# Loading the first feed-forward input tile ahead of the weight preparation instead of behind it

## The chip, the cores and the metric

One Trainium2 chip; the kernel runs on all 8 cores, each with 2 of the 16 sequences, and the cores don't talk to each other. The time is that of the slowest core, in microseconds (us) on the device. Each core has five engines: TensorE (PE, matmuls), VectorE (DVE), ScalarE (ACT), GpSimd (POOL) and SyncE (SP). In this kernel SyncE issues all loads and GpSimd all stores, each in the order of its program; an instruction that waits holds up all that follow it on its engine.

## The reference

The input X is (16, 2048, 1024) in float32. One attention layer is followed by a normalization, then by a three-block feed-forward part with 4-bit weights and LoRA, then by another normalization:

```python
x = _layernorm(x + attn(x, Wq, bq, Wk, bk, Wv, bv))     # causal, softmax over axis -2
# feed-forward: three blocks
w = q.astype(float32) / 7.5 - 1.0;  w = w * repeat(scale, 16, axis=1)      # dequantized weight
linear(x) = x @ w.T + bias + (x @ la.T) @ lb.T                             # LoRA of rank 32
h = x
for blk in range(3):
    y = gelu(layernorm(linear0(h)) * gamma + beta)
    h = linear1(y) + h
x = _layernorm(x + h)
```

## The kernel before, in words

One large buffer PL of 40,960 float32 columns per partition holds nearly everything; constants such as IBASE and O_WSTG are column offsets in it. Data is transposed: features on the partitions, tokens along the columns.

**Attention.** For each of the two sequences of a core: projections, scores, attention times values, residual sum. The stage ln1 then normalizes. Its result x1 (2048 tokens x 1024 features) lies in eight chunks of 128 x 2048 from offset 8192 on. VectorE normalizes chunks 0 to 4 (L624, L627) and GpSimd chunks 5 to 7 (L635, L638). After its own part GpSimd stores all eight chunks, 1 MB each, to the DRAM buffer x1s (L646). Where these stores stand is kept in sp_marks, one mark for each sequence.

**Weight preparation ("dequant").** dequant_w(w), for each of six weights: SyncE loads the LoRA factors (L666, L667), then for each of eight chunks c the quantized values (L693) and the scales (L696), 512 KB each. Three chunks are in flight: the loads of chunk c wait for VectorE's end of chunk c-3. ScalarE converts the integers (L713). TensorE makes the LoRA product of the chunk (L725, L727). VectorE multiplies by the scales (L739), adds the LoRA product (L743, L745), and GpSimd stores the finished bf16 chunk of 256 KB to the DRAM buffer weffs (L704). VectorE may write chunk c only when the store of chunk c-2 has landed, since the staging buffer has two places. The first loads of weight 0 wait for the last attention matmul, for the statistics of ln1 and for VectorE's count before it normalizes. They go to columns 24576 to 30720, which the x1 data (offsets 8192 to 24576) doesn't use.

**Feed-forward.** emit_group takes two tiles of 512 tokens each (t even and t odd). x1_load(t) loads a tile from x1s in eight DMAs of 256 KB (L801) into columns IBASE[t % 2] on. It waits for the last attention matmul or last use of the place, for sp_marks of both sequences, and for what it is given as extra. For tile 0 this is VectorE's end of the attention part, for tile 1 the end of dequant on all engines. w_load(j) loads prepared weight j, 2 MB in one DMA (L782). cast_in(t) makes the bf16 copy of the tile on VectorE (L815), which waits for the eight loads. y_mms makes the matmuls of a linear layer (L857) with statistics matmuls (L837, L839) between. It waits for the cast and the weight, and its bank guards make the third and fourth output block of the first tile wait for the end of dequant on VectorE.

Before the change the order on SyncE's queue around here is: all loads of dequant, x1_load(0), w_load(0), w_load(1), x1_load(1). VectorE's order is: normalization, dequant, cast of tile 0, cast of tile 1.

Of the kernel before, what the change touches and what calls it, by code (L numbers as in the profile page):

```python
# [72 lines left out]
def build_program():  # L73
# [23 lines left out]
    with ExitStack() as ctx:  # L97
# [42 lines left out]
        def inc(inst, name, n=1):  # L140
            cnt[name] += n
            inst.then_inc(sem[name], n)
            return cnt[name]

        def wt(e, name, v):
            e.wait_ge(sem[name], v)

        def chain(e, name):
            e.wait_ge(sem[name], cnt[name])
# [4 lines left out]
        def scope(name):  # L154
            sid, _ = nc.enter_named_scope(name, False)
            _scope_stack.append((name, sid))

        def escope():
            name, sid = _scope_stack.pop()
            nc.leave_named_scope(name, sid, False)  # L160
# [492 lines left out]
        attn_end = dict(cnt)  # L653
# [101 lines left out]
        IBASE = [8192, 8192 + 14336]  # L755
# [15 lines left out]
        def w_load(j):  # L771
            sl = j % 2
            nm = "lw%d" % sl
            free = wslot_pe[sl]
            swm = w_sw_marks[j]

            @blk.sync
            def _(e):
                wt(e, "pe", free)
                wt(e, "sw0", swm[0])  # L780
                wt(e, "sw1", swm[1])
                inc(e.dma_start(  # L782
                    out=bfv(WSL[sl], 8192).rearrange("p (c n) -> p c n", n=1024),
                    in_=weffs.ap()[j].rearrange("c p n -> p c n")), nm, 16)
            return (nm, cnt[nm])

        def x1_load(t, extra=()):
            i = t % 2
            seq_, off_ = t // (T // TT), (t % (T // TT)) * TT
            nm = "lf%d" % i  # L790
            free = inst_free_pe[i]

            @blk.sync
            def _(e):
                wt(e, "pe", free)
                for m in sp_marks:
                    wt(e, *m)
                for nm2, v2 in extra:
                    wt(e, nm2, v2)
                for c in range(EC):  # L800
                    inc(e.dma_start(out=fv(IBASE[i] + c * 512, 512),  # L801
                                    in_=x1s.ap()[seq_, c, :, off_:off_ + TT]), nm, 16)
            return (nm, cnt[nm])

        def cast_in(t, src_off, x1mark=None, extra=()):
            i = t % 2

            @blk.vector
            def _(e):
                if x1mark is not None:  # L810
                    wt(e, x1mark[0], x1mark[1])
                for nm2, v2 in extra:
                    wt(e, nm2, v2)
                chain(e, "ve")
                inc(e.tensor_copy(bfv(IBASE[i] + 12288, 4096), fv(src_off, 4096)), "ve")  # L815
            return ("ve", cnt["ve"])
# [161 lines left out]
        def ln_fin2(t, mu_copy=False):  # L978
            i = t % 2
            b0, b1 = (2, 3) if i == 0 else (6, 7)  # L980
            mcol = muB[:, i * 512:(i + 1) * 512]
            rcol = rsB[:, i * 512:(i + 1) * 512]
            ecol = e2s[:, i * 512:(i + 1) * 512]
            m2col = m2s[:, i * 512:(i + 1) * 512]
            p = cnt["pe"]

            @blk.scalar
            def _(e):
                wt(e, "pe", p)
                if mu_copy:  # L990
                    inc(e.copy(mcol, ps[b0][:]), "se")
                inc(e.activation(m2col, ps[b0][:], AF.Square), "se")
                inc(e.activation(ecol, ps[b1][:], AF.Copy, bias=EPS), "se")  # L993
            if mu_copy:
                stat_read[i] = ("se", cnt["se"])
            g1 = cnt["se"]

            @blk.vector
            def _(e):
                wt(e, "se", g1)  # L1000
                inc(e.tensor_sub(ecol, ecol, m2col), "ve")  # L1001
            g2 = cnt["ve"]

            @blk.scalar
            def _(e):
                wt(e, "ve", g2)
                inc(e.activation(m2col, ecol, AF.Ln), "se")
                chain(e, "se")
                inc(e.activation(rcol, m2col, AF.Exp, scale=-0.5), "se")
            return cnt["se"]  # L1010

        def apply_gelu(t, blki, fin):
            i = t % 2
            b0 = 2 if i == 0 else 6
            ybf = bfv(IBASE[i] + 4096, 4096)
            y3 = ybf.rearrange("p (x b) -> p x b", b=512)
            mub = bass.AP(ps[b0], 0, [[512, 128], [0, 8], [1, 512]])

            @blk.vector
            def _(e):  # L1020
                wt(e, "se", fin)
                chain(e, "ve")
                inc(e.tensor_sub(y3, y3, mub), "ve")  # L1023
                chain(e, "ve")
                inc(e.tensor_mul(y3, y3, bc512(rsB, i * 512)), "ve")  # L1025
            stat_read[i] = ("ve", cnt["ve"] - 1)
            am = cnt["ve"]

            @blk.scalar
            def _(e):  # L1030
                wt(e, "ve", am)
                for s in range(EC):
                    inc(e.activation(bfv(IBASE[i] + 6144, 4096)[:, s * 512:(s + 1) * 512],  # L1033
                                     ybf[:, s * 512:(s + 1) * 512], AF.Gelu,
                                     scale=gam[:, blki * 8 + s:blki * 8 + s + 1],
                                     bias=bet[:, blki * 8 + s:blki * 8 + s + 1]), "se")
            return ("se", cnt["se"])
# [76 lines left out]

        fbcols = [fb[:, w * 8:(w + 1) * 8] for w in range(6)]

        def emit_group(gname, ts, ex_x1=None, ex_cast=None, hook=None):
            nonlocal_osb = None
            scope(gname)
            xm = {}  # L1120
            wl = {}
            cm = {}
            for j in (0, 1):
                if hook:
                    hook(j)
            xm[ts[0]] = x1_load(ts[0], (ex_x1 or {}).get(ts[0], ()))
            wl[0] = w_load(0)
            wl[1] = w_load(1)
            for t in ts[1:]:
                xm[t] = x1_load(t, (ex_x1 or {}).get(t, ()))  # L1130
            for t in ts:
                cm[t] = cast_in(t, IBASE[t % 2], xm[t],
                                extra=(ex_cast or {}).get(t, ()))
            for blki in range(3):
                w1, w2 = 2 * blki, 2 * blki + 1
                gel = {}
                fin = {}
                for t in ts:
                    y_mms(t, w1, wl[w1], cm[t], "y1", fbcols[w1])
                    fin[t] = ln_fin2(t)  # L1140
                for t in ts:
                    gel[t] = apply_gelu(t, blki, fin[t])
                if w1 + 2 < 6:
                    if hook:
                        hook(w1 + 2)
                    wl[w1 + 2] = w_load(w1 + 2)
                for t in ts:
                    in1 = IBASE[t % 2] if blki == 0 else IBASE[t % 2] + 8192
                    tail = "cast" if blki < 2 else "r2"
                    cm[t] = y_mms(t, w2, wl[w2], gel[t], "y2",  # L1150
                                  (fbcols[w2], in1, tail))
                if w2 + 2 < 6:
                    if hook:
                        hook(w2 + 2)
                    wl[w2 + 2] = w_load(w2 + 2)
            for t in ts:
                ln_stats_r2(t, IBASE[t % 2] + 8192, cm[t][1])
            vo = {}
            for t in ts:
                fin2 = ln_fin2(t, mu_copy=True)  # L1160
                vo[t] = ln2_apply(t, fin2)
            for t in ts:
                globals_osb[0] = trans_store(t, vo[t])
            escope()

        globals_osb = [osb_sp]

        scope("dequant")
        for w in range(6):
            dequant_w(w)  # L1170
        escope()
        dq_end = dict(cnt)
        stat_read[1] = ("ve", dq_end["ve"])
        ygrp["guard"][4] = ("ve", dq_end["ve"])
        ygrp["guard"][5] = ("ve", dq_end["ve"])
        ex0 = {0: (("ve", attn_end["ve"]),),
               1: (("se", dq_end["se"]), ("ve", dq_end["ve"]),
                   ("gq0", dq_end["gq0"]), ("gq1", dq_end["gq1"]),
                   ("gq2", dq_end["gq2"]))}
        exc0 = {1: (("sw0", dq_end["sw0"]), ("sw1", dq_end["sw1"]))}  # L1180
        emit_group("ffng0", (0, 1), ex_x1=ex0, ex_cast=exc0)
        emit_group("ffng1", (2, 3))
        emit_group("ffng2", (4, 5))
        emit_group("ffng3", (6, 7))

# [60 lines left out]
```

## Time and profile before

| | |
|---|---|
| two timed runs | 2735.66 and 2911.03 us, median 2823.34 us |
| the profiled execution | 2729.84 us |
| its span, slowest core (of 2712.6 to 2728.2 us) | 2728.2 us |
| mean granted TensorE clock, core 7 | 0.800 of full speed |
| TensorE matmuls busy | 1656.4 us (61%) |
| VectorE busy | 1034.8 us (38%) |
| ScalarE busy | 1038.1 us (38%) |
| GpSimd busy | 131.0 us (5%) |

All rows are of core 7, the slowest, and start times count from the start of its span. A profile row of a stretch in order of time has: start, length, engine, line of the kernel, operation, target and sources, count, and in brackets how long the engine had been idle and what ended it. An engine name with a q (SPq) is the engine's queue at work on an instruction that isn't counted as busy, such as issuing a DMA. A line "DMA to landing" tells how long the DMAs of that line and stretch took from issue until they had landed: least, median, most.

### The profile page before, as it was taken

What the parts mean: (1) busy time and instruction counts of PE and PEld (TensorE: products, weight loads), DVE (VectorE), ACT (ScalarE), POOL (GpSimd) and SP (SyncE); (2) the same over time, 40 slices, a digit from 0 to 9 for tenths busy, and PEclk for the clock granted to TensorE, in tenths of its full rate; (3) what the DMA queues carried; (4) which work ended last, traced back from release to release, by engine and by line L of the source; (5) the groups of instructions that cost most, each with busy time, mean ns of one, the idle gap of its engine ahead of it and who ended that gap; (6) DMA issues with size and microseconds to landing.
All of it is one profiled execution on the core that took longest, in us unless ns stands there. A gap on an engine that the chain in (4) does not pass through costs nothing.

```text
span 2728.2 us, 21892 instructions; the slowest of 8 cores (2712.6 to 2728.2 us)
## 1 busy us (share of the span) xinstructions
PE 1656.4 (61%) x6880; PEld 689.0 (25%) x6880; DVE 1034.8 (38%) x1001; ACT 1038.1 (38%) x1517; POOL 131.0 (5%) x112
## 2 busy tenths in 40 slices
PE   0999881396989111115766566676467656665853
PEld 0444330143433000002322222232123222222321
DVE  2113435301343744441542724246323526152262
ACT  0421114242111312224454454444554464546444
POOL 0000003300000511010000000000000000000000
PEclk9999896698999555558888867898589887787985
DMA  6200134501012277673100050100330100511001
GB/s 189 96 35 16 47 108 154 185 16 54 16 47 78 77 257 258 232 256 117 58 31 31 0 185 31 62 31 0 98 118 31 38 24 6 180 50 43 31 1 62
DMA packets 72542, 228.62 MB, mean 84 GB/s; under 512 B 6768, under 2 KB 7024, under 8 KB 66032
## 3 DMA queue, kind: packets, MB, share of 16 engines
q1 hardware_dynamic: 61680, 181.09, 20.1%
q0 software_dynamic: 10752, 46.14, 4.4%
q8 instruction: 60, 0.98, 0.1%
q14 instruction: 50, 0.41, 0.1%
HBM read 181.07 MB, written 46.14 MB: 83 GB/s over the span
## 4 chain that ended last, share of the span: by engine, by line
PE 48%; ACT 16%; DVE 13%; DMA 11%; issue 8%; PEld 2%; DVEq 1%; PEldq 1%; SPq 0%; ACTq 0%; POOL 0%; POOLq 0%
PE ps L857 24%; PE ps L298 8%; PE ps L420 5%; DMA weffs<-PL 4%; PE ps L361 4%; ACT PL L1033 3%; PE ps L837 2%; PEld ps L496 2%; PE ps L1085 2%; DVE PL L1025 2%; DVE PL L1023 2%; DVE PL L627 2%; DVE PL L624 2%; DMA PL<-xt 2%; PE ps L839 2%
## 5 line engine op out<-in xcount | busy, mean ns | idle before, releaser
L857 PE MATMUL ps<-PL 128*128 128x512 bf16 x3072 | 738.5, 397 | 259.3 <-ACT PL L1033 237.6
L857 PEld LDWEIGHTS ps<-PL 128*128 128x128 bf16 x3072 | 310.3, 102 | 666.4 <-issue 339.9
L298 PE MATMUL ps<-PL 128*128 128x512 bf16 x1024 | 228.0, 386 | 170.2 <-DVE PL L214 66.6
L1001 DVE TENSOR_TENSOR e2s<-e2s,m2s 128x512 f32<-128x512 f32 x32 | 22.1, 692 | 546.8 <-ACT e2s L993 546.8
L725 PE MATMUL ps<-PL 32*128 32x512 bf16 x48 | 28.1, 585 | 279.5 <-DVEq L748 255.8
L880 ACT ACTIVATE PL<-ps,fb 128x512 bf16<-128x512 f32 x192 | 132.2, 688 | 165.2 <-PE ps L839 164.9
L893 DVE SCALAR_TENSOR_TENSOR PL<-ps,fb,PL 128x512 f32<-128x512 f32 x192 | 144.2, 751 | 90.1 <-PE ps L857 89.6
L298 PEld LDWEIGHTS ps<-PL 128*128 128x128 bf16 x1024 | 101.1, 99 | 296.6 <-issue 181.2
L1085 PE MATMUL ps<-eye,PL 128*128 128x128 f32 x256 | 88.0, 437 | 141.9 <-ACT PL L1099 76.8
L496 PE MATMUL ps<-PL 128*128 128x512 bf16 x640 | 142.6, 387 | 20.2 <-ACTq L173 20.2
L837 PE MATMUL ps<-PL,ones_b 128*128 128x512 bf16 x192 | 76.5, 399 | 119.0 <-ACT sqd L883 119.0
L420 PE MATMUL ps<-PL 128*128 128x512 bf16 x640 | 140.9, 382 | 7.8 <-issue 5.2
L377 DVE TENSOR_TENSOR PL<-ps,PL 128x512 bf16<-128x512 f32 x64 | 44.3, 692 | 257.7 <-PE ps L361 255.7
L1033 ACT ACTIVATE PL<-PL,bet,gam 128x512 bf16<-128x512 bf16 x192 | 138.2, 802 | 0.3
L883 ACT ACTIVATE sqd<-PL 128x512 bf16<-128x512 bf16 x192 | 121.1, 631 | 18.5 <-ACT PL L880 1.1
L361 PE MATMUL ps<-PL 128*128 128x512 bf16 x512 | 112.9, 384 | 21.9 <-ACTq L173 21.9
L713 ACT ACTIVATE PL<-PL 128x1024 f32<-128x1024 int32 x48 | 50.7, 1057 | 180.9 <-DMA PL<-sc_t 180.8
L739 DVE TENSOR_TENSOR PL<-PL 128x1024 f32<-128x1024 f32 x48 | 58.8, 1226 | 146.9 <-DMA weffs<-PL 85.6
L880 ACT ACT_TABLE_LOAD x24 | 30.8, 1283 | 213.8 <-PE ps L857 213.6
L1025 DVE TENSOR_TENSOR PL<-PL,rsB 128x4096 bf16<-128x4096 bf16 x24 | 106.2, 4425 | 2.8 <-DVE PL L1023 0.5
L1023 DVE TENSOR_TENSOR PL<-PL,ps 128x4096 bf16<-128x4096 bf16 x24 | 106.1, 4421 | 2.5
L1085 PEld LDWEIGHTS ps<-eye,PL 128*128 128x128 f32 x256 | 45.8, 180 | 184.9 <-issue 179.7
(80 smaller groups left out, 1727.3 us busy)
## 6 DMA issues: line engine op xcount, KB each, us to landing
PL<-weffs SPq DMA_DIRECT2D x24, 2048.0 KB, 9.5
PL<-xt SPq DMA_DIRECT2D x32, 1024.0 KB, 5.2
PL<-qw_t SPq DMA_DIRECT2D x48, 512.0 KB, 5.1
PL<-sc_t SPq DMA_DIRECT2D x48, 512.0 KB, 6.5
x1s<-PL POOLq DMA_DIRECT2D x16, 1024.0 KB, 11.5
PL<-x1s SPq DMA_DIRECT2D x64, 256.0 KB, 7.8
out<-PL POOLq DMA_DIRECT2D x32, 512.0 KB, 3.8
weffs<-PL POOLq DMA_DIRECT2D x48, 256.0 KB, 6.1
```

Source lines behind the costliest of these rows:

```text
L298: last = e.matmul(ps[bank][:], bfv(area + c * 512, 1024)[:, s * 128:(s + 1) * 128], xtbf[:, c * 2048 + tc * 512:c * 2048 + (tc + 1) * 512] ...
L361: last = e.matmul(ps[bank][:], xtbf[:, c * 2048 + ts * 128:c * 2048 + ts * 128 + 128], bfv(O_WBFA + c * 512, 1024)[:, hh * 512:(hh + 1) * ...
L420: last = e.matmul(ps[base + ic][:], kt[:, c * 2048 + jc * 128:c * 2048 + jc * 128 + 128], qt[:, c * 2048 + ic * 512:c * 2048 + (ic + 1) * ...
L496: last = e.matmul(ps[base + ic][:], bfv(O_VV + jc * 512, 1024)[:, es * 128:es * 128 + 128], ppseg(jc)[:, (ic - ic0) * 512:(ic - ic0 + 1) * ...
L837: e.matmul(ps[b0][:], ones_b[:], src_sum, start=(s_ == 0), stop=(s_ == EC - 1))
L857: last = e.matmul(ps[bank][:], bfv(WSL[sl], 8192)[:, c * 1024 + s * 128:c * 1024 + (s + 1) * 128], src_mv[:, c * 512:(c + 1) * 512], start ...
L880: inc(e.add(ybf[:, s * 512:(s + 1) * 512], ps[YB[(g0 + s) % 4]][:], evac_args[:, s:s + 1]), "se")
L893: inc(e.scalar_tensor_tensor(fv(IBASE[i] + 8192 + s * 512, 512), ps[YB[(g0 + s) % 4]][:], fbcol[:, s:s + 1], fv(in1_off + s * 512, 512), A ...
L1023: inc(e.tensor_sub(y3, y3, mub), "ve")
L1025: inc(e.tensor_mul(y3, y3, bc512(rsB, i * 512)), "ve")
L1033: inc(e.activation(bfv(IBASE[i] + 6144, 4096)[:, s * 512:(s + 1) * 512], ybf[:, s * 512:(s + 1) * 512], AF.Gelu, scale=gam[:, blki * 8 + s ...
L1085: inc(e.transpose(ps[bank][:, 0:128], fv(xo + c * 512 + tsl * 128, 128), eye[:]), "pe")
```

## The change

The load of tile 0 and its cast move from the start of the first feed-forward group to the place before the weight preparation. The waits of the load are the same as before; emit_group gets what was loaded already as `pre` and leaves it out. Everything else keeps its order. SyncE's order becomes: x1_load(0), all loads of dequant, w_load(0), w_load(1), x1_load(1). VectorE's order becomes: normalization, cast of tile 0, dequant, cast of tile 1. The buffers are the same: tile 0 at columns 8192 to 12288, its bf16 copy at 20480 to 22528, neither of which dequant writes.

```diff
-        def emit_group(gname, ts, ex_x1=None, ex_cast=None, hook=None):
+        def emit_group(gname, ts, ex_x1=None, ex_cast=None, hook=None,
+                       pre=None):
             nonlocal_osb = None
             scope(gname)
-            xm = {}
+            xm = dict((t, m[0]) for t, m in (pre or {}).items())
             wl = {}
-            cm = {}
+            cm = dict((t, m[1]) for t, m in (pre or {}).items())
...
-            xm[ts[0]] = x1_load(ts[0], (ex_x1 or {}).get(ts[0], ()))
+            if ts[0] not in xm:
+                xm[ts[0]] = x1_load(ts[0], (ex_x1 or {}).get(ts[0], ()))
             wl[0] = w_load(0)
             wl[1] = w_load(1)
             for t in ts[1:]:
-                xm[t] = x1_load(t, (ex_x1 or {}).get(t, ()))
+                if t not in xm:
+                    xm[t] = x1_load(t, (ex_x1 or {}).get(t, ()))
             for t in ts:
-                cm[t] = cast_in(t, IBASE[t % 2], xm[t],
-                                extra=(ex_cast or {}).get(t, ()))
+                if t not in cm:
+                    cm[t] = cast_in(t, IBASE[t % 2], xm[t],
+                                    extra=(ex_cast or {}).get(t, ()))
...
+        xm0 = x1_load(0, (("ve", attn_end["ve"]),))
+        cm0 = cast_in(0, IBASE[0], xm0)
+
         scope("dequant")
         for w in range(6):
             dequant_w(w)
...
-        ex0 = {0: (("ve", attn_end["ve"]),),
-               1: (("se", dq_end["se"]), ("ve", dq_end["ve"]),
+        ex0 = {1: (("se", dq_end["se"]), ("ve", dq_end["ve"]),
                    ("gq0", dq_end["gq0"]), ("gq1", dq_end["gq1"]),
                    ("gq2", dq_end["gq2"]))}
         exc0 = {1: (("sw0", dq_end["sw0"]), ("sw1", dq_end["sw1"]))}
-        emit_group("ffng0", (0, 1), ex_x1=ex0, ex_cast=exc0)
+        emit_group("ffng0", (0, 1), ex_x1=ex0, ex_cast=exc0,
+                   pre={0: (xm0, cm0)})
```

## Rows read from the trace of the kernel before

**Rows 1.** Spans and clocks of the cores: the slowest core.
```profile
core 7: 2728.2 us, clock 0.800
```

**Rows 2.** Stretches: busy us (x count) of PE, PEld, DVE, ACT, POOL; clock, DMA share.
```profile
1018.00:1231.00 213.00, 37.64 (x76) 5.60 (x76) 100.39 (x120) 59.35 (x55) 21.05 (x39) 0.50 0.72 246
1231.00:1243.00 12.00, 0.39 (x2) 0.15 (x3) 2.29 (x1) 0.00 (x0) 0.54 (x1) 0.50 0.98 297
```

**Rows 3.** Order of time on VectorE: scale multiplies of weights 0, 1 and 5.
```profile
958.42 1.23 DVE L739 TENSOR_TENSOR PL<-PL 128x1024 f32<-128x1024 f32 x1 [0.41 <-issue]
...
982.36 1.23 DVE L739 TENSOR_TENSOR PL<-PL 128x1024 f32<-128x1024 f32 x1 [18.30 <-DMA weffs<-PL]
...
1017.92 1.23 DVE L739 TENSOR_TENSOR PL<-PL 128x1024 f32<-128x1024 f32 x1 [10.18 <-ACT PL L713]
...
1194.68 1.23 DVE L739 TENSOR_TENSOR PL<-PL 128x1024 f32<-128x1024 f32 x1 [9.95 <-ACT PL L713]
```

**Rows 4.** Order of time on SyncE's queue: first chunk loads of weights 0, 1.
```profile
910.41 0.35 SPq L693 DMA_DIRECT2D PL<-qw_t  x1
...
1007.86 0.35 SPq L693 DMA_DIRECT2D PL<-qw_t  x1
```

**Rows 5.** Order of time on GpSimd: stores of x1, sequence 1.
```profile
958.59 2.10 POOL L646 DMA_DIRECT2D x1s<-PL  x4 [4.29 <-DVEq L629]
```

**Rows 6.** Line 646, last two stores of sequence 1 (959.6 to 960.2 us).
```profile
DMA to landing us min/median/max: 18.0/19.4/20.9
```

**Rows 7.** Line 646, last four stores of sequence 0: order of time, landing.
```profile
505.35 2.10 POOL L646 DMA_DIRECT2D x1s<-PL  x4 [4.29 <-DVEq L629]
...
DMA to landing us min/median/max: 10.7/13.1/16.0
```

**Rows 8.** Order of time, second group: loads of tile 2, weights, cast.
```profile
1588.02 5.43 SPq L801 DMA_DIRECT2D PL<-x1s  x8
1593.66 1.74 SPq L782 DMA_DIRECT2D PL<-weffs  x2
...
1601.11 2.35 DVE L815 CAST PL<-PL 128x4096 bf16<-128x4096 f32 x1 [20.20 <-DMA PL<-x1s]
```

**Rows 9.** Order of time on SyncE's queue between dequant and the first group.
```profile
1217.04 0.43 SPq L696 DMA_DIRECT2D PL<-sc_t  x1
1217.74 4.97 SPq L801 DMA_DIRECT2D PL<-x1s  x8
1222.92 2.56 SPq L782 DMA_DIRECT2D PL<-weffs  x2
1231.13 13.94 SPq L801 DMA_DIRECT2D PL<-x1s  x8
```

**Rows 10.** Order of time: casts of tiles 0, 1 and their first matmuls.
```profile
1233.20 2.29 DVE L815 CAST PL<-PL 128x4096 bf16<-128x4096 f32 x1 [2.35 <-DMA PL<-x1s]
1242.61 5.06 PE L857 MATMUL ps<-PL 128*128 128x512 bf16 x16 [21.62 <-DMA PL<-weffs]
...
1255.55 2.29 DVE L815 CAST PL<-PL 128x4096 bf16<-128x4096 f32 x1 [20.05 <-DMA PL<-x1s]
...
1265.02 3.61 PE L857 MATMUL ps<-PL 128*128 128x512 bf16 x16
```

**Rows 11.** The chain that ended last, 955 to 1235 us: start, length, what.
```profile
1008.25 6.89 DMA PL<-sc_t
```

**Rows 12.** Line 782, weight loads 0 (1222.9 us) and 1 (1223.8 us).
```profile
L782 SPq DMA_DIRECT2D PL<-weffs x2: 700/1178/1657, 1222.9 to 1223.8; - x2
DMA to landing us min/median/max: 19.3/22.6/25.8
```

**Rows 13.** Line 782, the same two loads in the second group (1593.7, 1594.2 us).
```profile
DMA to landing us min/median/max: 16.7/22.0/27.3
```

**Rows 14.** Line 696, the last load of scales (1217.0 us).
```profile
DMA to landing us min/median/max: 5.5/5.5/5.5
```

**Rows 15.** Line 782, all 24 weight loads of the kernel.
```profile
DMA to landing us min/median/max: 8.9/9.5/28.0
```

## The prediction

> **What bounds the kernel now.** The span of the slowest core is 2728.2 us and the profiled execution is put at 2729.84 us, so 1.6 us lie outside the span [rows 1]. The two timed runs are 2735.66 and 2911.03 us, with 2823.34 as their median. My sum is made against 2729.84 us, which is within 0.2% of the lower of the two and 3.3% under their median. I forecast an execution of the profiled kind.
>
> I first read the busy time of each engine in stretches, to find the stage that the change is in. The weight preparation ("dequant") runs from about 958 us to 1231 us. In its steady part TensorE works only 37.6 of 213 us and VectorE 100.4 of 213 us, while the DMA engines are busy 72% of the time; then there are 12 us in which TensorE has 0.4 us of work and the DMA engines are 98% busy [rows 2]. The stage is bound by its chain of load, convert, multiply, add and store, and both of its ends are bound by transfers. Nothing of the feed-forward groups runs beside it. So a microsecond by which its first multiply comes later goes into the end of the kernel in full, and so does one by which the first matmul of the first group comes sooner. The change touches just these two ends.
>
> Next I read VectorE in order of time [rows 3]. The multiply of chunk 0 of weight 0 starts at 958.42 us and that of chunk 1 right behind it, but that of chunk 2 only at 982.36, after 18.30 us in which it waited for a store of the prepared weight. That store (chunk 0's, on GpSimd's queue) stands behind the eight 1 MB writes of x1 for sequence 1. So the early start at 958 us is worth less than it looks. From weight 1 on, the rhythm is steady: first multiplies at 1017.92 (weight 1) and 1194.68 us (weight 5), 176.76 us for four weights, or 44.19 us each. Counted back from weight 1, weight 0 behaves as if it had started at 1017.92 - 44.19 = 973.73 us. This is the number to compare the new start with, not 958.42.
>
> **Part 1, the entry: the moved x1 load is now ahead of all of dequant on SyncE's queue.** Before, SyncE issued the LoRA loads and three chunk pairs at about 910 us, beside VectorE's layer norm [rows 4]. After, x1_load(0) comes first in that queue, with its waits for the landed x1 writes of both sequences (sp_marks) and for attn_end. Its eight loads then issue, then the two LoRA loads, then the first pairs. Behind the waiting SyncE stand all the loads of dequant; ScalarE's conversion waits for those, and VectorE's multiply for ScalarE. VectorE itself has the cast of tile 0 first, which waits for the eight loads. GpSimd's order isn't changed.
>
> - *When SyncE is released.* The last four writes of x1 are issued in 2.10 us from 958.59, the last at about 958.59 + 2.10 - 0.53 = 960.16 us [rows 5], and it lands 20.9 us later, at 981.1 us [rows 6]. Two pairs of chunk loads and two stores of weights run beside it now and won't after. The same writes for sequence 0, without those, have the last issue at 506.92 and landed 16.0 us after it [rows 7]. I take 960.16 + 16.0 = 976.2 us. Bounds: 970.9 (10.7 us, the least of the last four there) and 981.1.
> - *The x1 load.* From the first issue to the cast that waits for all eight: 1588.02 to 1601.11 us = 13.1 us in the next group [rows 8], and 1217.74 to 1233.20 us = 15.5 us here [rows 9, 10]. I take 13.1: the data is there at 989.3, and the cast of 2.29 us [rows 10] ends at 991.6 us.
> - *The first chunk.* SyncE needs 4.97 us for the eight issues [rows 9] and about 1 us for the LoRA ones, so the first pair is issued at 976.2 + 6.0 = 982.2 us. For weight 1 the multiply starts 1017.92 - 1007.86 = 10.1 us after the first issue of its pair [rows 3, 4]; that would give 992.3 us. But 2 MB of x1 are in front here and land at 989.3. The pair is 1 MB, half of what x1 moves in 9.3 us of my estimate for 2 MB (the lag worked out in part 2), so 4.6 us more; for weight 1 the scales of chunk 0 landed at 1008.25 + 6.89 = 1015.1 us [rows 11] and the multiply came 2.8 us later, which is ScalarE's table load and conversion. Sum: 989.3 + 4.6 + 2.8 = 996.7 us. The cast is done by then and is hidden by the wait for the pair; without that cover it would cost 2.3 us.
> - *Delay of the stage:* 996.7 - 973.7 = 23.0 us. Low bound, all in the cheap way: 970.9 + 6.0 + 10.1 = 987.0, that is 13.3 us. High bound: 981.1 + 15.5 + 4.6 + 2.8 = 1004.0, that is 30.3 us. From there on weight 0 has the rhythm of weights 1 to 5, since the store that chunk 2 waits for no longer stands behind the x1 writes; the other 47 chunks just move.
>
> **Part 2, the exit: eight loads and a cast are gone from between dequant and the first matmul.** Before, SyncE issues the last pair at 1217.04, the eight x1 loads from 1217.74, and w_load(0) only at 1222.92 us [rows 9]. The cast runs from 1233.20 to 1235.5 and isn't what is late: the first matmul starts at 1242.61 us [rows 10], when the 2 MB of w_load(0) have landed, 19.3 us after issue, at 1242.2 us [rows 12]. That is 9.0 us after x1 landed (1233.2). In the next group the weights land at 1593.66 + 16.7 = 1610.4 us, 9.3 us after x1 (1601.11) [rows 8, 13]. So what is gained isn't the cast (2.3 us, hidden under the weights already) but that the weights move up to x1's place: issued at 1217.7, with only the last pair ahead, which landed 5.5 us after 1217.04 [rows 14], at 1222.5 us. Add 9.2 us: landed at 1231.7, first matmul at 1232.1 instead of 1242.6, a gain of 10.5 us. Nothing else holds it: its first two output blocks use banks that are free, and the third waits for VectorE's end of dequant at about 1231.1 us, which is over when it gets there. Low bound of the gain: only the 5.2 us by which the issue comes sooner (same 19.3 us in flight). High bound: the shortest landing of such a load, 8.9 us [rows 15], that is 1226.6 us and a gain of 15.6 us.
>
> The Trainium skill (DMA: Bandwidth & Descriptors, Anatomy of one DMA) fits a single DMA as 2.0 us plus bytes over 436,000 per us. For 2 MB that is 6.8 us, where the row has 8.9 us at least [rows 15]; with it the weights would land at 1229.3 us, the gain would be 12.9 us and the total 2740 us. The rows are of this kernel with all eight cores running, so they decide.
>
> What is late next is tile 1: its load still waits for the end of dequant (1231.13) and its cast started at 1255.55 us, under the matmuls of tile 0, with those of tile 1 following at 1265.02 us [rows 9, 10]. Moved up by 10.5 us these would start at 1254.5 us. The second weight load landed at 1223.8 + 25.8 = 1249.6 us [rows 12] and the x1 data 5.9 us behind it; with the queue 10.5 us ahead the cast starts at about 1245 us and ends at 1247.4. It stays hidden with some 7 us to spare. Left where it is, it would end at 1257.8, and 3.3 us of the gain would be lost.
>
> **Sum.** 2729.84 + 23.0 - 10.5 = 2742.3 us. With the bounds: 13.3 - 15.6 = -2.3 us to 30.3 - 5.2 = +25.1 us, or 2728 to 2755 us.
>
> **The rivals.**
>
> - *Faster: the start of dequant was behind the x1 writes anyway.* In favour: the 18.30 us wait before chunk 2. If the new start costs nothing, only the exit counts: 2729.84 - 10.5 = 2719 us. It decides from the point where the first multiply comes at 973.7 + 10.5 = 984.2 us or sooner, so that SyncE would be released by 984.2 - 16.1 = 968.1 us, 7.9 us after the last x1 write is issued. The last write took 20.9 us here and 16.0 us for sequence 0, and even the first of the last four took 10.7 us. Chance 0.07.
> - *The exit gives nothing:* the DMA engines are 98% busy there, and were the weights held by something other than x1, the first matmul would stay at dequant's end plus 11.5 us: 2729.84 + 23.0 = 2753 us. Against it are the two equal lags of 9.0 and 9.3 us behind x1. Chance 0.12.
> - *The entry is dearer:* x1's loads are issued in one stretch, with others behind them. Tile 1's eight took 13.94 us to issue and 1255.55 - 1231.13 = 24.4 us to the cast [rows 9, 10], since 4 MB of weights were in flight. With that and the late release: 981.1 + 24.4 + 4.6 + 2.8 = 1012.9 us, 39.2 us of delay, and 2729.84 + 39.2 - 10.5 = 2759 us. Against it: there is nothing in front of them on that queue now. Chance 0.17.
> - *My forecast,* 2728 to 2755 us around 2742: chance 0.60. The other 0.04 I leave to what none of these name, half of it above 2784 us.
>
> **The numbers.** A difference of 2%, about what a measurement of this kernel can tell from no change, is 55 us: below 2675 or above 2784 us. None of the four cases reaches either, so within 2% has 0.95; slower by over 2% gets 0.03 for an entry that disturbs more than the first weight, and faster 0.02. The range goes from 2725 us (half of the faster rival left out) to 2772 us, past the dear entry by what differs from one execution to the next (the lower timed run is 6 us over the profiled one).
>
> **What would show it.** Right: no loads of the LoRA and chunk data at 910 us but after about 982; a cast between 989 and 992 us; the first multiply at 997 us; 44 us from weight to weight; the weight load issued right behind the last pair and the first matmul about 14.6 us after that issue instead of 24.9. It would be wrong if the first multiply came before 984 us (the entry was covered), if the first matmul still followed the last pair by 25 us (the exit wasn't held by x1), or if the first matmuls of tile 1 found their cast missing.

## The result, and the profile after

| | before | after |
|---|---|---|
| median of all timed runs | 2774.54 us (12 runs) | 2747.13 us (13 runs) |
| lowest | 2730.48 us | 2742.00 us |
| the profiled execution | 2729.84 us | 2745.49 us |
| after against before (ratio) | | 1.0048 (95% interval 1.0037 to 1.0060) |

The change makes the kernel 0.5% slower, 13.1 us of 2733. In some executions of either kernel the cores of one die show a lower granted clock and the time is 3 to 7% longer; the ratio and the 2733 us leave these out, and they are why the medians of all runs, 2774.54 and 2747.13, stand the other way round.

The profiled execution of the changed kernel is shown on its slowest core, core 3. There the last attention stage begins 1 us later than on core 7 of before. First SyncE's queue in order of time, which answers to [rows 4]: the x1 load, the LoRA loads, and weight 0's first pair.

```profile
975.38 4.33 SPq L801 DMA_DIRECT2D PL<-x1s  x8
979.86 0.68 SPq L666 DMA_DIRECT2D PL<-la_h  x1
...
981.14 0.55 SPq L693 DMA_DIRECT2D PL<-qw_t  x1
```

Then VectorE in order of time, which answers to [rows 3]: the cast of tile 0, the multiplies of chunks 0 and 2 of weight 0, and the first of weights 1 and 5. The ScalarE row between is the start of its work for weight 0.

```profile
988.01 2.29 DVE L815 CAST PL<-PL 128x4096 bf16<-128x4096 f32 x1 [29.04 <-DMA PL<-x1s]
989.87 1.28 ACT L674 ACT_TABLE_LOAD   x1 [79.53 <-DMA PL<-lb_h]
...
995.84 1.23 DVE L739 TENSOR_TENSOR PL<-PL 128x1024 f32<-128x1024 f32 x1 [5.54 <-ACT PL L713]
...
1004.88 1.23 DVE L739 TENSOR_TENSOR PL<-PL 128x1024 f32<-128x1024 f32 x1 [3.39 <-DMA weffs<-PL]
...
1039.34 1.23 DVE L739 TENSOR_TENSOR PL<-PL 128x1024 f32<-128x1024 f32 x1 [9.28 <-ACT PL L713]
...
1217.42 1.23 DVE L739 TENSOR_TENSOR PL<-PL 128x1024 f32<-128x1024 f32 x1 [9.46 <-ACT PL L713]
```

VectorE has nothing to do between the end of its layer norm (959 us) and the cast, 29.04 us. Chunk 2's wait for the store of chunk 0 has shrunk from 18.30 us to 3.39 us, so of the 37 us by which chunk 0 starts later only some 21 us are left at weight 1. ScalarE waits for the LoRA factors (lb_h) and not for the scales: it converts these factors first, and comes to the quantized values behind them. From weight 1 to weight 5 it is 178.1 us here and 176.8 us before.

The exit, in order of time on SyncE's queue, TensorE and VectorE, answering to [rows 9, 10]:

```profile
1239.73 0.43 SPq L696 DMA_DIRECT2D PL<-sc_t  x1
1240.37 2.14 SPq L782 DMA_DIRECT2D PL<-weffs  x2
1253.74 5.90 SPq L801 DMA_DIRECT2D PL<-x1s  x8
...
1255.95 5.78 PE L857 MATMUL ps<-PL 128*128 128x512 bf16 x16 [12.48 <-DMA PL<-weffs]
...
1270.79 2.29 DVE L815 CAST PL<-PL 128x4096 bf16<-128x4096 f32 x1 [17.33 <-DMA PL<-x1s]
...
1278.59 3.61 PE L857 MATMUL ps<-PL 128*128 128x512 bf16 x16
```

The first matmul comes 16.2 us after the last scale load's issue, where it was 25.6 us. The matmuls of tile 1 begin 22.6 us after those of tile 0, where it was 22.4 us: nothing new is in the way.

One slowest core against another mixes what the change does with what differs from core to core. So I read the same four marks on each of the 8 cores in each kernel's profiled execution and took medians. The marks are the first instruction of sequence 1's layer norm on VectorE, the first multiply of weight 1, that of weight 5, and the first matmul of the first group. All in us:

| kernel | layer norm to weight 1 | weight 1 to 5 | weight 5 to first matmul | from there to the end |
|---|---|---|---|---|
| before | 107.9 | 175.6 | 47.6 | 1483.7 |
| after | 129.1 | 175.9 | 37.8 | 1485.4 |
| e1_wait_only | 119.3 | 175.3 | 47.3 | 1484.8 |
| e2_after_reload | 128.7 | 175.7 | 47.8 | 1484.4 |
| e3_x1_mid | 108.8 | 174.9 | 37.2 | 1484.2 |
| e4_x1_w_mid | 108.7 | 178.7 | 26.9 | 1485.0 |
| e5_stores_early | 93.8 | 175.7 | 46.5 | 1484.5 |
| e6_after_stores | 117.2 | 177.4 | 37.5 | 1484.5 |
| e7_all | 96.2 | 178.8 | 26.4 | 1486.8 |
| e8_precise_wait | 128.8 | 175.0 | 38.1 | 1483.3 |
| e10_pairs_first | 109.0 | 174.6 | 37.3 | 1485.4 |
| e11_pairs_precise | 114.0 | 175.8 | 37.8 | 1483.4 |

(e9_all_again is the kernel of e7_all once more.)

The change costs 21.2 us at the entry and gives 9.8 us at the exit, 11.4 us net; 13.1 us were timed. The last column moves by 1 to 3 us in kernels that change nothing there, so that is how finely the table can be read.

### The profile page after: what moved, and what is told of

The parts are those of the page before. It is cut to its first block, busy times and chain, and to the rows that moved or that the text cites. A ratio compares the mean times of both kernels' runs of the same rounds, so it can differ in the third digit from the quotient of the medians.

```text
span 2743.9 us, 21892 instructions; the slowest of 8 cores (2725.9 to 2743.9 us)
## 1 busy us (share of the span) xinstructions
PE 1657.4 (60%) x6880; PEld 689.7 (25%) x6880; DVE 1034.7 (38%) x1001; ACT 1035.7 (38%) x1517; POOL 131.1 (5%) x112
## 4 chain that ended last, share of the span: by engine, by line
PE 48%; ACT 16%; DVE 13%; DMA 11%; issue 8%; PEld 2%; DVEq 1%; PEldq 1%; SPq 0%; ACTq 0%; POOL 0%; POOLq 0%
PE ps L857 24%; PE ps L298 8%; PE ps L420 5%; DMA weffs<-PL 4%; PE ps L361 4%; ACT PL L1033 3%; PE ps L837 2%; PEld ps L496 2%; PE ps L1085 2%; DVE PL L1025 2%; DVE PL L1023 2%; DMA PL<-xt 2%; DVE PL L627 2%; DVE PL L624 2%; PE ps L839 2%
```

## The experiments

Ratios are against the kernel before, run on the same chip beside them, with their 95% intervals; times in us are a ratio's difference from 1 times 2733 us.

My theory at this point had three parts. The entry costs because SyncE stands still until the last x1 store has landed (about 13 us). It costs because x1's 2 MB then pass in front (about 10 us). The exit gives what those 2 MB cost there (about 10 us).

**e1_wait_only.** In the kernel before:

```diff
         scope("dequant")
+        @blk.sync
+        def _(e):
+            for m in sp_marks:
+                wt(e, *m)
         for w in range(6):
```

> The kernel before, with SyncE waiting for the landed x1 stores ahead of dequant's first loads; the x1 load and its cast stay behind dequant. My theory (the entry of the change costs 23 us, of which the wait is about 13 and the x1 load's issue and 2 MB in front about 10; the exit gives about 10): first multiply of dequant at about 976 + 1 + 10 = 987 us against 973.7 us (counted back from weight 1), so 13 to 14 us over the kernel before. Rival A (the whole cost of the entry is the wait, and the bytes are free): first multiply at about 996 us as in the changed kernel, 22 us over the kernel before. Rival B (the start was covered by the x1 stores anyway): within 3 us of the kernel before.

Measured: 1.0050 (1.0035 to 1.0064), 13.7 us slower. On its slowest core, in order of time on SyncE's queue and VectorE:

```profile
974.54 0.34 SPq L666 DMA_DIRECT2D PL<-la_h  x1
...
975.49 0.35 SPq L693 DMA_DIRECT2D PL<-qw_t  x1
...
984.94 1.22 DVE L739 TENSOR_TENSOR PL<-PL 128x1024 f32<-128x1024 f32 x1 [26.43 <-ACT PL L713]
```

The first multiply comes at 984.94 us, 9.45 us after the first pair's issue. The entry costs 11.4 us by the table, so the wait alone is half of what the change pays. The whole change and the wait alone come to the same time, 13 us, because the x1 load costs about 10 us more at the front (129.1 against 119.3) and gives about 10 back at the end (37.8 against 47.3). Moving the load to the very front is worth nothing in itself, and the wait that comes with it is what is left over; e8 and e10 below say what it is in this wait that costs.

**e2_after_reload.** In the changed kernel, ahead of w_load(0), into columns unused at that time:

```diff
+            else:
+                @blk.sync
+                def _(e):
+                    for c in range(EC):
+                        inc(e.dma_start(
+                            out=fv(IBASE[0] + 8192 + c * 512, 512),
+                            in_=x1s.ap()[0, c, :, 0:TT]), "ld", 16)
...
-        exc0 = {1: (("sw0", dq_end["sw0"]), ("sw1", dq_end["sw1"]))}
+        exc0 = {1: (("ld", 128), ("sw0", dq_end["sw0"]), ("sw1", dq_end["sw1"]))}
```

> The changed kernel, with the same eight 256 KB loads of x1 issued once more (to unused columns) between the last pair of dequant and the first weight load; nothing waits for them but the cast of tile 1, which comes later. My theory (the exit gains because x1's issue and 2 MB were in front of the weight load): the gain goes, first matmul about 25 us after the last pair's issue, 9 to 11 us over the changed kernel and 23 us over the kernel before. Rival (the exit gained because the load and the cast of tile 0 were taken out of the waits, not because of the queue): no change against the changed kernel, within 2 us.

Measured: 1.0084 (1.0061 to 1.0107), 23.0 us over the kernel before. SyncE's queue and TensorE, in order of time:

```profile
1238.08 0.43 SPq L696 DMA_DIRECT2D PL<-sc_t  x1
1238.55 4.17 SPq L1133 DMA_DIRECT2D PL<-x1s  x8
1242.93 2.48 SPq L782 DMA_DIRECT2D PL<-weffs  x2
...
1263.92 4.87 PE L857 MATMUL ps<-PL 128*128 128x512 bf16 x15 [21.92 <-DMA PL<-weffs]
```

No matmul waits for these eight loads, and still the first comes 25.8 us after the last scale load's issue, as before the change. So the exit's gain is that the eight loads are gone from in front of the weight load, all of it (47.8 against 37.8 in the table). The run doesn't tell the 4.2 us of their issue from the 2 MB that they move.

**e3_x1_mid.** In the changed kernel the load stands behind weight 0 and the cast behind weight 1:

```diff
-        xm0 = x1_load(0, (("ve", attn_end["ve"]),))
-        cm0 = cast_in(0, IBASE[0], xm0)
         for w in range(6):
             dequant_w(w)
+            if w == 0:
+                xm0 = x1_load(0, (("ve", attn_end["ve"]),))
+            if w == 1:
+                cm0 = cast_in(0, IBASE[0], xm0)
```

> The x1 load of tile 0 stands on SyncE's queue after weight 0's loads instead of before them, and its cast on VectorE after weight 1. My theory (entry and exit are separate): the entry's 23 us are gone, the exit's 9 to 10 us stay, since the load falls into the idle time of the DMA engines between two weights: 8 to 11 us faster than the kernel before. Rival (2 MB more inside a stage that is 72% busy with transfers cost what they save at its end): within 3 us of the kernel before.

Measured: 0.9972 (0.9960 to 0.9985), 7.7 us faster, just short of my 8 to 11. Entry and exit are separate: 0.9 us is lost at the one and 10.4 us gained at the other. Put behind one weight, the same load is a gain.

**e4_x1_w_mid.** As e3, with the first two weight loads behind weights 2 and 3:

```diff
+            if w in (2, 3):
+                wl0[w - 2] = w_load(w - 2)
...
-            wl[0] = w_load(0)
-            wl[1] = w_load(1)
+            wl = dict(prew or {})
+            if not wl:
+                wl[0] = w_load(0)
+                wl[1] = w_load(1)
```

> As e3_x1_mid, and the first two weight loads of the first group are issued after the loads of weights 2 and 3. My theory: at the exit only TensorE's own order and VectorE's end of dequant are left; the first matmul starts at about 1226 us of the old count with its third block at 1231, 15 to 17 us faster than the kernel before (6 us faster than e3_x1_mid). Rival (each 2 MB load inside dequant holds up the pair behind it): no faster than e3_x1_mid, dequant's 44.2 us from weight to weight becoming 48 us or more for the weights with a load.

Measured: 0.9950 (0.9930 to 0.9969), 13.7 us faster. TensorE in order of time:

```profile
1224.26 0.63 PE L727 MATMUL ps<-PL 32*128 32x512 bf16 x1
1224.82 5.50 PE L857 MATMUL ps<-PL 128*128 128x512 bf16 x16
...
1232.34 1.89 PE L857 MATMUL ps<-PL 128*128 128x512 bf16 x8 [0.40 <-DVEq L748]
```

The first matmul follows the last LoRA matmul with no wait, and the third block waits 0.40 us for VectorE's end of dequant, both as forecast. I was 1.3 us short of my lower bound. The two 2 MB loads are not quite free inside dequant: 178.7 us from weight 1 to 5 against 175.6, and 178.8 in e7, which has them too.

**e5_stores_early.** In the kernel before, GpSimd issues the x1 stores between its own chunks, for both sequences; put(c) holds the old wait and store of chunk c:

```diff
                     inc(e.drain(), "gp")
-                for c in range(EC):
...
+                    put(c)
+                    put(c - 5)
+                put(3)
+                put(4)
```

> The kernel before, with GpSimd's eight x1 stores of each sequence issued between its own normalization chunks (5, 0, 6, 1, 7, 2, 3, 4) instead of all after them; the load of tile 0 stays behind dequant. My theory (weight 0 acts as started at 973.7 us because its stores stand behind the x1 stores): the last x1 store lands at about 965 us, chunk 2 isn't held up, dequant acts as started at 960 to 964 us, 10 to 13 us less; sequence 0 has the same stall ahead of its next projections and may give up to 12 us more: 10 to 25 us faster than the kernel before. Rival (the DMA engines set both and the stores only move): within 3 us.

Measured: 0.9930 (0.9914 to 0.9945), 19.1 us faster. VectorE in order of time, chunks 0 and 2 of weight 0:

```profile
950.80 1.23 DVE L743 TENSOR_TENSOR PL<-PL 128x1024 f32<-128x1024 f32 x1 [0.41 <-issue]
...
960.36 1.22 DVE L743 TENSOR_TENSOR PL<-PL 128x1024 f32<-128x1024 f32 x1 [3.91 <-DMA weffs<-PL]
```

Chunk 2 waits 3.91 us instead of 18.30. The stage gains 14.1 us from layer norm to weight 1. What sequence 0's earlier stores give is the rest, about 5 us, and less than the 12 I had allowed for. The traces bear it out: from the layer norm of sequence 0 to that of sequence 1 it is 448.2 us in e5 and 453.9 us before, as medians over the cores.

**e6_after_stores.** The changed kernel with the same edit.

> The changed kernel with those early stores. My theory (the entry of the change is release of SyncE by the last x1 store, then 20 us to the first multiply): released at about 965 us, first multiply at about 985 us instead of 996. Against the kernel with the early stores alone it is still 10 to 15 us slower (entry about 22 us, exit about 10 back). Rival (with the stores early the wait is over before VectorE is free, so the change is free at the entry): 8 to 10 us faster than the kernel with the early stores alone.

Measured: 0.9993 (0.9977 to 1.0009), which is 0.63% or 17 us over e5, 2 us beyond my range. The entry is 23.4 us dearer than e5's (117.2 against 93.8) and the exit 9.0 us cheaper. On its slowest core SyncE is released 54 us and the first multiply comes 74 us after the start of the layer norm (65 and 85 us in the changed kernel), so from the release to the multiply it is 20 us in both, as forecast. Earlier stores help both kernels and don't make the change free.

**e8_precise_wait.** The test of my theory's first part. The x1 load of tile 0 needs only sequence 0's stores, and of sequence 1 those whose columns it overwrites, so the wait can be narrowed (sp_marks[0] is sequence 0's, sp_marks[2] the new one for chunks 0 and 1 of sequence 1, "sx"; VectorE counts three for each of its five chunks, so attn_end["ve"] - 9 is its end of chunk 1):

```diff
-                        "sl%d" % seq, 16)
+                        "sx" if seq == 1 and c < 2 else "sl%d" % seq, 16)
...
-        xm0 = x1_load(0, (("ve", attn_end["ve"]),))
-        cm0 = cast_in(0, IBASE[0], xm0)
+        xm0 = x1_load(0, (("ve", attn_end["ve"] - 9),),
+                      marks=(sp_marks[0], sp_marks[2]))
...
+            if w == 0:
+                cm0 = cast_in(0, IBASE[0], xm0, extra=(sp_marks[1],))
```

> The changed kernel, but the x1 load of tile 0 at the front waits only for what it overwrites (the stores of sequence 1's chunks 0 and 1, which get a semaphore of their own) and for sequence 0's stores, and its cast stands behind weight 0 with a wait for all x1 stores. My theory (the change's net cost is that SyncE stands still until the last x1 store has landed; the load itself costs at the front what it gives at the end): SyncE is released at about 957 us instead of 975, its loads then run beside the stores, first multiply at about 980 to 985 us instead of 996, so 11 to 16 us faster than the changed kernel and within 5 us of the kernel before. Rival (the x1 load in front of dequant's loads is what costs, whenever it is released; beside the stores it only lands as late): first multiply at 992 us or later, no more than 5 us faster than the changed kernel.

Measured: 1.0037 (1.0019 to 1.0055), 10.1 us over the kernel before and only 3 us under the changed one, with intervals that overlap. My theory missed and the rival hit. SyncE's queue, ScalarE and VectorE in order of time:

```profile
958.35 5.35 SPq L802 DMA_DIRECT2D PL<-x1s  x8
...
965.20 1.86 SPq L697 DMA_DIRECT2D PL<-sc_t  x1
...
991.98 1.28 ACT L675 ACT_TABLE_LOAD   x1 [81.60 <-DMA PL<-lb_h]
...
997.95 1.23 DVE L740 TENSOR_TENSOR PL<-PL 128x1024 f32<-128x1024 f32 x1 [38.96 <-ACT PL L714]
```

SyncE is released at 958.35 us, 17 us sooner, and the first multiply is at 997.95 us, no sooner than after the change (995.84). The row of ScalarE names what it waits for, the LoRA factors (lb_h, issued at 964.24 us). They are under way for 27.7 us, and the scales of chunk 0 behind them for 29.5 us:

```profile
DMA to landing us min/median/max: 27.7/27.7/27.7
...
DMA to landing us min/median/max: 29.5/29.5/29.5
```

In the changed kernel the same two took 9.2 and 10.6 us. So the last 17 us of SyncE's standing still are not what costs: without them the transfers take as much longer. What is left in e8 is that SyncE stands still from 910 to 958 us and the first pairs miss their old time. The windows of the three kernels show what that time holds. The first row of each is 909 to 949 us, the second 949 to 981 us, and the last two numbers are the DMA engines' share and GB/s. Before:

```profile
909.00:949.00 40.00, 1.86 (x4) 0.42 (x4) 38.80 (x7) 8.12 (x8) 37.62 (x6) 0.50 0.24 85
949.00:981.00 32.00, 2.01 (x4) 0.27 (x4) 13.68 (x10) 1.06 (x1) 5.36 (x10) 0.50 0.97 322
```

After:

```profile
909.00:949.00 40.00, 0.00 (x0) 0.00 (x0) 37.83 (x7) 1.35 (x1) 37.02 (x6) 0.50 0.00 0
949.00:981.00 32.00, 0.00 (x0) 0.00 (x0) 9.62 (x4) 0.00 (x0) 4.86 (x9) 0.50 0.84 286
```

e8_precise_wait:

```profile
909.00:949.00 40.00, 0.00 (x0) 0.00 (x0) 37.80 (x7) 1.38 (x1) 36.98 (x6) 0.50 0.00 0
949.00:981.00 32.00, 0.00 (x0) 0.00 (x0) 9.64 (x4) 0.00 (x0) 4.91 (x9) 0.50 0.95 278
```

Before the change 3.4 MB (85 GB/s for 40 us) pass between 909 and 949 us, beside the layer norm, when nothing else uses the DMA engines. The change leaves these 40 us empty. In e8 the loads fall into the stretch that is full of x1 stores instead, and in the changed kernel they come behind it. The Trainium skill (DMA: Bandwidth & Descriptors, Queues, rings and completion order) says that each DMA engine takes turns between the queues that have work for it. The rows fit that: beside the loads the last x1 store took 24.8 us to land in e8, against 14.1 us in the changed kernel, where no loads ran beside the stores.

**e10_pairs_first.** The test of this second theory. Only weight 0's LoRA loads and first three pairs go back ahead of the x1 load, which keeps its full wait (mid() calls it for weight 0):

```diff
+                for c in range(3):
...
+            if mid:
+                mid()
+            @blk.sync
+            def _(e):
+                for c in range(3, EC):
```

> The changed kernel, but weight 0's LoRA loads and its first three pairs keep their old place at about 910 us, ahead of the x1 load with its old waits; the pairs 3 to 7 stand behind it, and the cast behind weight 0. New theory, after e8_precise_wait fell short (what the entry costs is that the pairs lose the idle time of the DMA engines at 910 us and queue behind 10 MB of stores and x1): chunks 0 to 2 start as before (958, 961, 982 us), pair 3 is issued at about 981 us and its multiply starts at 995 to 997 us, against 985 in the kernel before and 1010 in the changed one: entry 9 to 12 us over the kernel before, exit 10 less, so within 4 us of the kernel before. Rival (an x1 load ahead of dequant's loads costs 20 us wherever the first pairs stand): 8 us or more over the kernel before.

Measured: 0.9975 (0.9961 to 0.9989), 6.8 us faster than the kernel before. The entry costs 1.1 us instead of 21.2, with the x1 load and its wait still ahead of 45 of the 48 pairs. VectorE in order of time, chunks 2 and 3:

```profile
974.00 1.23 DVE L753 TENSOR_TENSOR PL<-PL 128x1024 f32<-128x1024 f32 x1 [11.52 <-DMA weffs<-PL]
...
990.95 1.23 DVE L753 TENSOR_TENSOR PL<-PL 128x1024 f32<-128x1024 f32 x1 [14.34 <-ACT PL L727]
```

The new theory holds, and I had even set the entry 8 to 11 us too dear, which is also why the time lies outside my "within 4 us". Chunk 2 comes 17.2 us after chunk 0 (956.83), where it was 23.9 us in the kernel before: pairs 3 and 4 no longer run beside the x1 stores, the last of which lands after 14.7 us instead of 20.9. I had expected it where it was. Chunk 3 comes 34.1 us after chunk 0 where it was 27.0 us in the kernel before. Pairs 4 and 5, which then wait for nothing, are issued right behind pair 3, so chunks 4 to 7 catch up; I had left that out too. What no run tells apart is the early issue of the three pairs and the idle engines that they meet: none issues them early into a full stretch.

**e11_pairs_precise.** Both together: early pairs and the narrow wait.

> As e10_pairs_first with the x1 load's waits of e8_precise_wait (released at about 957 us, beside the stores). By the new theory the DMA engines are full from 950 to 981 us, so 2 MB more in that stretch move what follows by 6 to 8 us wherever they are released: entry 5 to 9 us, exit 10 less: 1 to 5 us faster than the kernel before. Rival (the wait of SyncE is what costs, and it is now gone): entry 0 to 2 us, 8 to 10 us faster than the kernel before.

Measured: 0.9985 (0.9974 to 0.9997), 4.1 us faster, entry 6.1 us. To release the x1 load beside the stores is 5 us dearer at the entry than to let it wait (114.0 against 109.0), although SyncE is released some 18 us sooner, counted from chunk 0's multiply (1.3 us ahead of it against 16.6 us behind it). On VectorE chunk 2 now waits twice as long for its store as in e10 (11.52 us):

```profile
992.30 1.23 DVE L754 TENSOR_TENSOR PL<-PL 128x1024 f32<-128x1024 f32 x1 [23.56 <-DMA weffs<-PL]
```

The timed ratios lean the same way but their intervals overlap.

**e7_all and e9_all_again.** e4 and e5 together, and the same kernel once more in more rounds.

> e4_x1_w_mid and e5_stores_early together. My theory (the two are at different ends of dequant and add up): 25 to 40 us faster than the kernel before, the sum of the two measured apart. Rival (the earlier stores are what makes room for the mid-stage loads, or the reverse): less than the sum by 5 us or more.

> The kernel of e7_all once more, in more rounds, since its 26 us and the sum of its two halves (33 us) lie within each other's intervals. If the halves add up: 30 us or more faster than the kernel before. If they get in each other's way: 24 to 28 us again, and the medians over the cores show more than 3 us of loss from weight 1 to the first matmul against e4_x1_w_mid.

Measured: 0.9906 (0.9886 to 0.9926) and 0.9899 (0.9876 to 0.9922), 25.7 and 27.6 us faster than the kernel before, and 1.4 to 1.5% faster than the changed kernel. It is the fastest version here. The two halves measured apart add up to 32.8 us. In the table e7 loses 2.4 us to weight 1 against e5 (e4 loses 0.8 us there against the kernel before) and nothing after it against e4 (205.2 against 205.6 us from weight 1 to the first matmul). So the loss after weight 1 that I named as a sign is not there. The spans of the timed runs say where the 5 to 7 us are missing. On the median core e4 saves 12.6 us, e5 19.4 us and both together 31.7 us (29.4 us in the repeat), so there the halves add up or nearly. What is missing is on the slowest core, which sets the time; the intervals of the four ratios allow chance, and its cause stays open.

## Why the prediction was right or wrong

**The total.** The sum of the text, 12.5 us over the profiled execution of before, met 13.1 us timed, and 2742 us stands 5 us under the median of all runs of the changed kernel. What failed is the step at the start, "My sum is made against 2729.84 us": the sum took this as the time of the kernel before, and the forecast was left to stand beside the times shown. With 2823.34 us as the median shown, a forecast of 2742 us reads as 3% faster, while the text forecast half a per cent slower; I named the gap and didn't resolve it. The six lowest of the 12 timed runs of before, 2730.48 to 2735.66 us, show that the profiled execution was the right base, and against it the change is slower, by a ratio of 1.0048. Two runs that are 175 us apart could not show it, and the direction should have been stated as a difference: about 0.5% slower.

**The release of SyncE.** Forecast 976.2 us, measured 975.38. The last x1 store landed 14.1 us after its issue, where I had taken 16.0 from sequence 0.

**The x1 load and the cast.** Forecast 13.1 us from first issue to cast; measured 12.6. The cast was hidden, as forecast: it ended at 990.3 us and the multiply came at 995.84.

**The first multiply.** Forecast 996.7 us, measured 995.84 us; delay of the stage forecast 23.0, measured 21.2 as a median over the cores. That the time is so close is in part luck. The scales of chunk 0 landed at 992.3 us, 1.6 us sooner than my 993.9. From there to the multiply it was 3.5 us and not 2.8, since ScalarE was still at the LoRA factors, which landed at 989.8 us; my sum had no term for their conversion. The two errors nearly cancel.

**What that delay is made of was only half right.** This is where the mechanism failed, though the number held. I put it on two things in a row, SyncE's wait and the load in front, and found the times of both. But the step "behind the waiting SyncE stand all the loads of dequant" names the wait as the price, and e8 took 17 us of the wait away for 3 us or less. The price is that weight 0's first pairs lose their early place, an empty stretch of the DMA engines; with it given back and the whole wait kept, the entry costs 1.1 us (e10). My rows had it: in [rows 4] the first pair is issued at 910 us, 48 us ahead of its use, and I used this row only for its old place, never asking what those transfers would meet at their new one. In this kernel both readings give one number, because the wait ends when the engines come free.

**The exit.** Forecast 10.5 us, measured 9.8. The first matmul came 15.6 us after the weight load's issue (14.6 forecast, 19.7 before; the 24.9 that the forecast sets beside it counts from x1's first issue). The weights landed 15.2 us after issue, and 9.9 us behind the last pair (1239.73 + 6.0 = 1245.7), where I had 9.2. e2 shows the cause directly. The Trainium skill's fit (DMA: Bandwidth & Descriptors, Anatomy of one DMA), 2.0 us plus bytes over 436,000, would have had 6.8 us there; the trace doesn't agree with it. The fit is for one DMA on GpSimd's path, and this one is SyncE's, with others around it.

**Tile 1.** Its cast started 14.8 us after the first matmul, where I had 12.9. It ended at 1273.1 us, 5.5 us ahead of tile 1's matmuls at 1278.59, and stayed hidden as forecast (7 us to spare).

**The rivals.** The free entry was wrong and would have needed the first multiply by 984 us. The exit that gives nothing was wrong: it gave 9.8 us. The dear entry with 24.4 us for the load didn't come: the load took 12.6 us, with the x1 stores landed and nothing in front of it on SyncE's queue.

## What to carry to other kernels

When a load moves forward past others in a queue, ask of each load that it is moved past which transfers it ran beside at its old place and which it will meet at the new one. An idle stretch of the DMA engines that was given up here cost 20 of the entry's 21 us, and shortening the wait in front of the loads didn't bring it back (e10, e8). Put an extra load behind the ones that use such a stretch (e10, e3), not ahead of them. Moving the same bytes from the end of this transfer-bound stage to its very front was worth nothing (e1 against the change); behind its first loads or in its middle they were a gain (e10, e3).

## What the runs showed that I had not expected

- Taking a wait away can cost: with the x1 load released some 18 us sooner, beside the stores, the way to weight 1 took 114.0 us against 109.0 (e11 and e10).
- The order in which finished chunks are stored was worth more than the change studied here: 19.1 us, by issuing the same eight stores between GpSimd's computations instead of after them (e5).
- Three pairs issued back to back let the stage catch up: in e10 chunk 3 is 7 us later than in the kernel before, counted from chunk 0, and weight 1 only 1.1 us.
